# Reordered loads at the start and a reordered meeting of two stages in an AdaLN/FFN kernel on one core

## The chip, the cores and the metric

The kernel runs on one core of a Trainium2 chip. Its time is the device time of one execution, in microseconds; the median of several executions counts. The engines are TensorE (PE; its weight loads are listed apart as PEld), VectorE (DVE), ScalarE (ACT), GpSimd (POOL) and SyncE (SP), which here only issues transfers.

## The reference

x is (32, 64, 1024): 2048 tokens of 1024 features. It goes through two residual stages.

```python
x = x + L0_ffn(L0_cond(x))     # stage 0
x = x + L1_ffn(L1_cond(x))     # stage 1
# L0_cond: agg_w[b] = softmax(mlp(cond[b])) . weight[k];  out = agg_w @ x + agg_b   (64 x 64 per batch)
# L0_ffn:  r = softmax(x @ gate_w.T); ((x * (r @ in_scale)) @ sign(W).T) * (r @ out_scale) + bias
# L1_cond: grouped convolution, 4 groups, 9 taps over the 1024 positions, + ctx + bias
# L1_ffn:  x @ W.T + b, plus 8 gated low-rank terms: w_e = softmax_e(q_e . k_e), h_e = x @ A_e.T, sum of w_e h_e @ B_e.T
```

Everything is float32. Products are made in a reduced format from split operands: each float32 operand is a rounded high part and a rest (`hi`, `lo`), and two or three products of parts stand for one.

## The kernel before

The tokens are 16 tiles of 128 rows (two batches each), handled as 8 pairs; tile (i, p) is tile 2i + p. Every buffer that a tile needs exists twice, one for each p. Each engine has its own program written out in order, with loops over the pairs in the middle and the first and last pairs unrolled; the engines meet only through semaphores, on which an instruction waits until a count is reached. So an instruction that waits holds up all that stands behind it on its engine.

**Stage 0, one tile on PE**: `product_y` (64 small products, L425, bank from `agg` and the x tile in `xs`), `product_logits` (L438), `sum_logits` (L448), `turn_routing` (L455), `product_scales` (L467 and L473) and 32 `ffn0_step`s of 128x512 (L491). The small products of later tiles are put between the steps of the current one at fixed step numbers (`TURN_AT`, `BLOCK_AT`, `SUM_AT`). The first tile has its own list (k = 6, 10, 16, 22, 28): at k == 22 PE waits for the fourth tile of x, tile (1, 1), with `inputs_of_y(1, 1)`, and only then makes the logits of tile (1, 0). DVE adds the mix bias (L883), scales (L905), makes the rests (L912) and multiplies with the out scale (L920, semaphore `scaled`). POOL adds the bias row `bias_bc` to the second copy of x (`add_bias0`, L1059), adds the product (`make_x1`, L1066), and makes the rest of each chunk of `wearly`, the first weights of stage 1 (`rest_of_stage`, L1070). ACT rounds (`round_parts` L724, `round_stage` L738).

**SP, the one queue of nearly all transfers**: `load_next(i, p, biased)` waits until the tile that had the buffer has been used (`y_biased`), loads x into `xs` (L227) and the row for it (L232). `load_again(i, p)` loads x a second time into `resid`, which is part of `work` (L266); in the first pair these buffers held parts of the sign weights, so it waits for `signs_ready`. `replace_x1` stores the result of stage 0 to memory (`x1_scratch`, L287) and loads the next tile into the same buffer. `next_chunk` loads the next chunk of `wearly` once the last is split. `load_raw` (L336) reads a finished tile of `x1_scratch` back as 8 transfers into `raw`, the convolution's input.

**Where the stages meet**: in the last tile of stage 0, PE puts the first convolution (`product_conv(0, 2)`, 128 small products, L566) in front of step `CONV0_AT`. DVE adds the context (L991, L995) into `z_t`, ACT rounds it and DVE makes the rests (semaphores `z_biased`, `z_hi`, `z_lo`). PE then waits for `stage_hi[0]` and `stage_lo[0]` to reach 8 (all chunks of `wearly` split) and for `z_lo`, and starts `period1`: 48 steps of 128x320 (L587, q, k and A), the next convolution, 24 steps of 128x512 with `early`, the transposed gates and 24 steps with `late` weights that are themselves split only then (`late_hi` on ACT L801, `late_lo` on DVE L1008 and POOL L1096). After that all tiles run the same `period1`.

Of the kernel before, what the change touches and what calls it, by code (L numbers as in the profile page):

```python
# [32 lines left out]
P = 128  # L33
B, S, H = 32, 64, 1024
TILES = B * S // P
PAIRS = TILES // 2
L8 = H // P
# [19 lines left out]

TURN_AT, BLOCK_AT, SUM_AT, CONV0_AT = 7, 18, 26, 8
LORA_AT = 11
# [4 lines left out]
def adaln_ffn_kernel(nc, x, consts, rows, mix, wsign, scales, bias0, toep, wearly, wlate, bm, bias1, out):  # L64
# [6 lines left out]
    with ctx:  # L71
# [153 lines left out]
        def _(sp):  # L225
# [42 lines left out]
            sp.wait_ge(rows_stored, 16)  # L268
            load_next(1, 0, 2)
            for p in range(2):  # L270
                sp.wait_ge(signs_ready, 7 + p)
                load_again(0, p)
            sp.wait_ge(scale_ready, 1)
            sp.dma_start(bias_bc[:, :], bias0.broadcast_to([P, H])).then_inc(bias0_loaded, 16)
            load_next(1, 1, 4)

# [30 lines left out]

            late_i, last = PAIRS - 3, PAIRS - 1
            load_next(last, 1, 4 * late_i + 8)
            replace_x1(late_i, 0)  # L310
            next_chunk(late_i)
# [14 lines left out]

            def load_raw(i, p):

                sp.wait_ge(x1_stored[p], 16 * (i + 1))
                src = tile_rows(x1_dram, 2 * i + p).rearrange("(n c) (l q) -> l c n q", c=CG, l=L8)  # L330
                half = L8 // 2
                for lo in range(2):
                    for l in range(half):
                        part = (lo * half + l) * CG
                        at = 1 - lo
                        sp.dma_start(raw[part:part + CG, p, :, at:at + P],  # L336
                                     src[(1 - lo) * half + l]).then_inc(raw_loaded[p], 16)

            sp.wait_ge(pads_zeroed, 2)
            load_raw(0, 0)  # L340
            load_raw(0, 1)
# [40 lines left out]
        def _(pe):  # L382
# [206 lines left out]
            def period1(i, p, ni, q, late_ready=None):  # L589
# [4 lines left out]
                for h in range(2):  # L594
                    for k in range(24):
                        if h == 1 and k == 12 and ni is not None:
                            inputs_of_conv(ni, q)
                            if late_ready:

                                pe.wait_ge(out_scale_ready, 2 * TILES)  # L600
                            else:

                                pe.wait_ge(out_ready, 4 * i + 2 * p)
                        last = z_step(bank[2 + h][:, 0:NH], lambda b, c: early[:, b, c, h * NH:(h + 1) * NH], p, k)
                    last.then_inc(qk_done, 1)
# [28 lines left out]

            pe.wait_ge(stage_hi[0], 8)
            pe.wait_ge(stage_lo[0], 8)
            pe.wait_ge(stage_hi[1], 1)
# [27 lines left out]
        def _(act):  # L665
# [126 lines left out]
            period0(last, 0, (last, 1))  # L792
            period0(last, 1, None, None, last)

            act.wait_ge(ffn0_done, 2 * TILES - 2)
            round_parts(0, 0, z_t, z_biased, z_hi, by_token)

            act.wait_ge(ffn0_done, 2 * TILES)
# [256 lines left out]
        def _(pool):  # L1055
# [15 lines left out]


            def period0(before, now, chunk=None):

                make_x1(*before, 1)
                add_bias0(*now)
                if chunk is not None:
                    hi, lo = (early[:, a, bass.ds(chunk, 1), :].rearrange("p a n -> p (a n)") for a in range(2))
                    rest_of_stage(0, NW, chunk + 1, lo, hi)
                make_x1(*now, 0)  # L1080
# [6 lines left out]
            rest_of_stage(1, H, 1, lora[:, 1, :], lora[:, 0, :])  # L1087
            with pool.Fori(1, PAIRS) as i:
                period0((i - 1, 1), (i, 0))
                period0((i, 0), (i, 1), i)  # L1090
            last = PAIRS - 1
            make_x1(last, 1, 1)
            for k in (0, 2):
# [89 lines left out]
```

## Time and profile before

| what | value |
|---|---|
| median of 3 runs | 557.45 us (555.99 to 559.61) |
| the profiled execution | 560.03 us, of it span 558.0 us |
| PE busy | 538.6 us, 97% of the span |
| PEld, DVE, POOL, ACT busy | 83%, 46%, 28%, 22% |
| chain that ended last | PE 92%, DVE 3%, DMA 2%, ACT 1%, issue 1% |
| mean granted clock of PE | 0.991 |

The chain is followed back from the last instruction to what released it at each step. PE's busy time says that it had a matmul in flight; how fast those ran depends on the granted clock, which the views by windows give as a share of full speed.

### The profile page before, as it was taken

Reading aid. Unit: us, or ns where it says so; the run is one execution under the profiler, and the core shown is the slowest. Engines: PE = TensorE matmul, PEld = TensorE weight load, DVE = VectorE, ACT = ScalarE, POOL = GpSimd, SP = SyncE. Lnnn points to the kernel's source line nnn. Section 1 sums busy time; section 2 is a strip of 40 time slices with the busy share of each in tenths; the row PEclk is TensorE's granted clock in tenths of the full one; section 3 lists DMA queues with packets and bytes.
Section 4 is the critical chain, followed back from the end, with each engine's and each line's share of the span. In section 5 each row is a group of like instructions: output and inputs, shape, how many; then the busy total and the mean of one; then the engine's idle time right before and its main releaser. Section 6 shows DMA issues by size and latency. Waiting matters only on the chain.

```text
span 558.0 us, 13990 instructions
## 1 busy us (share of the span) xinstructions
PE 538.6 (97%) x5717; PEld 461.9 (83%) x5717; DVE 254.7 (46%) x461; ACT 123.4 (22%) x289; POOL 155.5 (28%) x79
## 2 busy tenths in 40 slices
PE   5879999999999899999999999999999999999997
PEld 4657788787887798898988988989889899898896
DVE  4439888797775762323224332242232322422321
ACT  5614434343434320101101011011011110110100
POOL 0027776767758490110101101011011010110100
PEclk9989999999999989999999999999999999999999
DMA  8684565555558451330412303204033032130100
GB/s 311 241 330 159 172 204 187 197 197 187 204 172 215 132 185 43 81 104 17 119 51 66 117 14 103 95 22 118 38 80 113 4 118 78 40 118 39 39 39 38
DMA packets 38775, 66.79 MB, mean 120 GB/s; under 512 B 4384, under 2 KB 25056, under 8 KB 38752
## 3 DMA queue, kind: packets, MB, share of 16 engines
q1 hardware_dynamic: 38528, 66.09, 36.3%
q10 hardware_dynamic: 224, 0.36, 0.3%
q8 instruction: 19, 0.31, 0.2%
q14 instruction: 4, 0.03, 0.0%
HBM read 49.64 MB, written 16.79 MB: 119 GB/s over the span
## 4 chain that ended last, share of the span: by engine, by line
PE 92%; DVE 3%; DMA 2%; ACT 1%; issue 1%; SPq 0%; DVEq 0%; ACTq 0%
PE bank L587 52%; PE bank L491 19%; PE bank L566 8%; PE bank L622 4%; PE bank L425 3%; DMA xs<-in_x 2%; PE bank L438 2%; PE bank L467 2%; DVE parts L912 1%; DMA cst<-in_consts 1%; ACT late L693 1%; PE bank L448 0%; PE bank L455 0%; PE bank L473 0%; ACT parts L724 0%
## 5 line engine op out<-in xcount | busy, mean ns | idle before, releaser
L587 PE MATMUL bank<-early,parts 128*128 128x320 f32 (+1 forms) x1152 | 208.2, 339 | 1.8 <-DVE parts L912 1.8
L587 PEld LDWEIGHTS bank<-early,parts 128*128 128x128 f32 x1152 | 186.1, 189 | 18.7 <-issue 2.2
L491 PE MATMUL bank<-late,parts 128*128 128x512 f32 x512 | 131.1, 408 | 1.5 <-ACT parts L724 1.5
L1101 POOL TENSOR_TENSOR work<-work,bias_bc 128x1024 f32<-128x1024 f32 x16 | 38.0, 2375 | 279.2 <-DMA work<-x_scratch 279.2
L491 PEld LDWEIGHTS bank<-late,parts 128*128 128x128 f32 x512 | 95.0, 193 | 22.6 <-ACT parts L724 1.7
L587 PE MATMUL bank<-late,parts 128*128 128x512 f32 x384 | 94.1, 394 | 0.0
L587 PEld LDWEIGHTS bank<-late,parts 128*128 128x128 f32 x384 | 70.9, 188 | 15.9
L912 DVE TENSOR_TENSOR parts<-y_t,parts 128x512 fp32r<-128x512 f32 x64 | 59.4, 931 | 12.3 <-ACT parts L724 11.0
L724 ACT ACTIVATE parts<-y_t 128x512 fp32r<-128x512 f32 x64 | 39.7, 633 | 98.7 <-DVE y_t L995 67.0
L1066 POOL TENSOR_TENSOR work<-work 128x512 f32<-128x512 f32 x32 | 45.9, 1436 | 49.4 <-DVE work L920 48.2
L1016 DVE TENSOR_TENSOR qk<-bank,qk 128x256 f32<-128x256 f32 x16 | 6.8, 425 | 104.6 <-ACT qk L810 104.6
L1059 POOL TENSOR_TENSOR work<-work,bias_bc 128x1024 f32<-128x1024 f32 x16 | 42.4, 2651 | 38.1 <-DMA bias_bc<-in_bias 33.8
L566 PEld LDWEIGHTS bank<-band,raw 64*64 64x64 f32 x2048 | 44.3, 134 | 3.2 <-issue 3.2
L566 PE MATMUL bank<-band,raw 64*64 64x128 f32 (+1 forms) x2048 | 46.5, 246 | 0.0
L1045 DVE TENSOR_TENSOR work<-bank,work 128x512 f32<-128x512 f32 x32 | 22.0, 688 | 41.0 <-PE bank L622 41.0
L1035 DVE TENSOR_TENSOR wh_t<-bank,wh_t 128x128 fp32r<-128x128 f32 x16 | 4.7, 292 | 76.0 <-ACT wh_t L818 76.0
L905 DVE TENSOR_TENSOR y_t<-bank,y_t 128x512 f32<-128x512 f32 x32 | 20.6, 686 | 26.7 <-PE bank L467 26.7
L808 ACT ACTIVATE qk<-bank 128x64 f32<-128x64 f32 x16 | 3.6, 223 | 111.2 <-PE bank L587 111.2
L622 PE MATMUL bank<-lora,wh_t 128*128 128x512 f32 x96 | 27.7, 396 | 0.0
L734 ACT ACTIVATE work<-bank 128x512 f32<-128x512 f32 x32 | 18.7, 587 | 23.8 <-POOL work L1066 23.8
L920 DVE TENSOR_TENSOR work<-bank,work 128x512 f32<-128x512 f32 x32 | 21.7, 681 | 4.7 <-PE bank L491 4.7
L991 DVE TENSOR_TENSOR y_t<-bank,row_bc 128x512 f32<-128x512 f32 x32 | 22.0, 688 | 3.5 <-PE bank L566 3.1
(91 smaller groups left out, 351.0 us busy)
## 6 DMA issues: line engine op xcount, KB each, us to landing
xs<-in_x SPq DMA_DIRECT2D x16, 512.0 KB, 3.4
work<-in_x SPq DMA_DIRECT2D x16, 512.0 KB, 3.3
x_scratch<-work SPq DMA_DIRECT2D x16, 512.0 KB, 3.0
raw<-x_scratch SPq DMA_DIRECT2D x128, 64.0 KB, 3.0
work<-x_scratch SPq DMA_DIRECT2D x16, 512.0 KB, 3.7
out_tokens<-work SPq DMA_DIRECT2D x15, 512.0 KB, 2.7
stage<-in_wearly SPq DMA_DIRECT2D x8, 576.0 KB, 3.9
row_bc<-token_rows_scratch SPq DMA_DIRECT2D x30, 64.0 KB, 3.2
```

Source lines behind the costliest of these rows:

```text
L491: last = mm(bank[4 + h][:, :], parts[:, p, a, c, :], signs[:, c, h * HALF:(h + 1) * HALF], start=(k % 16 == 0), stop=(k % 16 == 15))
L566: last = mm(into[g * S:(g + 1) * S, at + cols.start:at + cols.stop], raw[rows, p, n, s + g * S:s + (g + 1) * S], band[rows, s * GROUPS + n ...
L587: return mm(dst, parts[:, p, a, c, :], w(b, c), start=(k == 0), stop=(close and k == 23))
L622: last = mm(o[h][:, :], wh_t[:, a, :], lora[:, b, h * HALF:(h + 1) * HALF], start=False, stop=(k == 2))
L724: do(cols(parts[:, p, 0], h), cols(src, h), ACT.Copy).then_inc(done, 1)
L912: v.tensor_tensor(cols(parts[:, p, 1], h), cols(src, h), cols(parts[:, p, 0], h).bitcast(F32), ALU.subtract).then_inc(done, 1)
L920: v.tensor_tensor(o, bank[4 + h][:, :], o, ALU.mult).then_inc(scaled, 1)
L991: v.tensor_tensor(zt, by_group(bank[h]), add.broadcast_to([P, 4, L8, CG]), ALU.add).then_inc(conv_halved, 1)
L1045: v.tensor_tensor(o, bank[4 + 2 * p + h][:, :], o, ALU.add).then_inc(out_ready, 1)
L1059: g.tensor_tensor(resid[:, p, :], resid[:, p, :], bias_bc[:, :], ALU.add).then_inc(xb_ready, 2)
L1066: g.tensor_tensor(resid[:, p, cols], os_sb[:, cols], resid[:, p, cols], ALU.add).then_inc(x1_ready, 1)
L1101: g.tensor_tensor(resid[:, p, :], resid[:, p, :], bias_bc[:, :], ALU.add).then_inc(resid_ready, 1)
```

## The change

Four things are moved; nothing is computed that was not computed before.

- SP, start: the bias row and then `load_next(1, 1, 4)` are issued in front of the two `load_again(0, p)`, which were in front.
- SP, last pairs: `load_raw(0, 0)` is issued right behind the last `load_next`, that is in front of `replace_x1(5, 0)`; `load_raw(0, 1)` stays.
- PE: `CONV0_AT` is 4 instead of 8. The wait for the eighth chunk of `wearly` stands in front of step 21 of the first 24 steps of `period1` instead of in front of its first step, where 7 chunks are now enough.
- ACT and POOL, last pair: ACT rounds `z_t` of tile (0, 0) ahead of its work for stage 0's last tile and of the rounding of the last chunk. POOL waits for `z_lo` and splits the last chunk ahead of `add_bias0(7, 1)`; before, the chunk came behind it and waited for nothing but its rounding.

```diff
-TURN_AT, BLOCK_AT, SUM_AT, CONV0_AT = 7, 18, 26, 8
+TURN_AT, BLOCK_AT, SUM_AT, CONV0_AT = 7, 18, 26, 4
...
             load_next(1, 0, 2)
+            sp.wait_ge(scale_ready, 1)
+            sp.dma_start(bias_bc[:, :], bias0.broadcast_to([P, H])).then_inc(bias0_loaded, 16)
+            load_next(1, 1, 4)
             for p in range(2):
                 sp.wait_ge(signs_ready, 7 + p)
                 load_again(0, p)
-            sp.wait_ge(scale_ready, 1)
-            sp.dma_start(bias_bc[:, :], bias0.broadcast_to([P, H])).then_inc(bias0_loaded, 16)
-            load_next(1, 1, 4)
...
+            load_next(last, 1, 4 * late_i + 8)
             sp.wait_ge(pads_zeroed, 2)
             load_raw(0, 0)
+            replace_x1(late_i, 0)
+            next_chunk(late_i)
+            replace_x1(late_i, 1)
...
                     for k in range(24):
+                        if late_ready and h == 0 and k == 21:
+
+                            pe.wait_ge(stage_hi[0], 8)
+                            pe.wait_ge(stage_lo[0], 8)
...
-            pe.wait_ge(stage_hi[0], 8)
-            pe.wait_ge(stage_lo[0], 8)
+            pe.wait_ge(stage_hi[0], 7)
+            pe.wait_ge(stage_lo[0], 7)
...
-            period0(last, 1, None, None, last)
-
             act.wait_ge(ffn0_done, 2 * TILES - 2)
             round_parts(0, 0, z_t, z_biased, z_hi, by_token)
+            period0(last, 1, None, None, last)
...
-            with pool.Fori(1, PAIRS) as i:
+            with pool.Fori(1, PAIRS - 1) as i:
                 period0((i - 1, 1), (i, 0))
                 period0((i, 0), (i, 1), i)
             last = PAIRS - 1
+            period0((last - 1, 1), (last, 0))
+            make_x1(last, 0, 1)
+            pool.wait_ge(z_lo, 2)
+            split_chunk(last)
+            add_bias0(last, 1)
+            make_x1(last, 1, 0)
             make_x1(last, 1, 1)
```

How the instructions move on SP at the start of the program (the names are those above; `work<-in_x` is `load_again`, `xs<-in_x` the x tile of `load_next`; - is before, + is after):

```order
 L227 DMA xs<-in_x 128x1024
 L232 DMA row_bc<-token_rows_scratch 128x128
-L266 DMA work<-in_x 128x1024 x2
-L274 DMA bias_bc<-in_bias 128x1024
+L271 DMA bias_bc<-in_bias 128x1024
 L227 DMA xs<-in_x 128x1024
 L232 DMA row_bc<-token_rows_scratch 128x128
+L266 DMA work<-in_x 128x1024 x2
 L235 DMA stage<-in_bm 128x1024
 L235 DMA stage<-in_wearly 128x1152
```

The second `xs<-in_x` is the fourth tile of x; three transfers stood between it and the first, now one does, the bias row.

On POOL at the end of stage 0, before (the loop's last rows, and what followed it):

```order
L1059 TENSOR_TENSOR work<-work,bias_bc 128x1024
L1070 ISA
L1070 TENSOR_TENSOR early<-stage,early 128x1152
L1064 REGISTER_ALU
L1066 TENSOR_TENSOR work<-work 128x512
L1088 REGISTER_ALU
L1088 COMPARE_AND_BRANCH
L1066 TENSOR_TENSOR work<-work 128x512
L1096 TENSOR_TENSOR late<-late_raw,late 128x1024
L1096 TENSOR_TENSOR late<-stage,late 128x1024
```

and with the change, behind the loop that is now one round shorter:

```order
L1069 TENSOR_TENSOR work<-work 128x512
L1062 TENSOR_TENSOR work<-work,bias_bc 128x1024
L1069 TENSOR_TENSOR work<-work 128x512 x2
L1073 TENSOR_TENSOR early<-stage,early 128x1152
L1062 TENSOR_TENSOR work<-work,bias_bc 128x1024
L1069 TENSOR_TENSOR work<-work 128x512 x2
L1108 TENSOR_TENSOR late<-late_raw,late 128x1024
L1108 TENSOR_TENSOR late<-stage,late 128x1024
```

The split (`early<-stage,early`) of the last chunk now stands in front of the last bias addition (`work<-work,bias_bc`), not behind it.

## Rows read from the trace of the kernel before

**Rows 1.** Waits: engine and line, what it waited for; total us, times, longest.

```profile
PE bank L438 <- DMA xs<-in_x: 4.1, 1, 4.1
```

**Rows 2.** Timeline from the start: start us, us, engine, line, instruction, count.

```profile
22.11 1.28 DVE L883 TENSOR_TENSOR y_t<-bank,row_bc 128x512 f32<-128x512 f32 x2
...
23.93 1.27 SPq L266 DMA_DIRECT2D work<-in_x  x2
...
29.54 1.64 PE L491 MATMUL bank<-late,parts 128*128 128x512 f32 x6
...
30.33 0.33 SPq L227 DMA_DIRECT2D xs<-in_x  x1
```

**Rows 3.** Chain that ended last, in order of time: start us, us, what.

```profile
25.72 9.55 DMA xs<-in_x
...
35.96 1.63 PE bank L425 x64
...
38.63 2.86 PE bank L491 x6
...
58.98 1.09 PE bank L425 x64
...
60.67 2.02 PE bank L491 x8
```

**Rows 4.** Windows: us, busy (instructions) by engine, granted clock PEclk, DMA share, GB/s.

```profile
36.00:43.00 7.00, 7.00 (x86) 5.89 (x86) 3.21 (x7) 2.24 (x7) 1.83 (x2) 0.52 0.75 298
196.00:200.20 4.20, 4.20 (x20) 4.20 (x19) 4.20 (x4) 1.67 (x2) 4.09 (x3) 0.59 0.09 37
```

**Rows 5.** Timeline, DVE, after the fourth tile of x.

```profile
38.66 1.29 DVE L905 TENSOR_TENSOR y_t<-bank,y_t 128x512 f32<-128x512 f32 x2 [7.50 <-PE bank L467]
...
45.14 0.68 DVE L920 TENSOR_TENSOR work<-bank,work 128x512 f32<-128x512 f32 x1
```

**Rows 6.** Transfers issued at 20 to 23, 25.1 to 25.6 and 30 to 40 us; last, us to landing.

```profile
xs<-in_x SPq DMA_DIRECT2D x1, 512.0 KB, 3.3
...
bias_bc<-in_bias SPq DMA_DIRECT2D x1, 512.0 KB, 8.7
...
xs<-in_x SPq DMA_DIRECT2D x1, 512.0 KB, 9.2
```

**Rows 7.** Timeline from 146 to 174 us, SP and POOL, the last pairs of stage 0.

```profile
151.02 0.33 SPq L266 DMA_DIRECT2D work<-in_x  x1
...
159.22 2.40 POOL L1059 TENSOR_TENSOR work<-work,bias_bc 128x1024 f32<-128x1024 f32 x1
...
173.88 8.82 SPq L336 DMA_DIRECT2D raw<-x_scratch  x16
```

**Rows 8.** Timeline from 179 us on, where the stages meet.

```profile
179.94 5.29 PE L491 MATMUL bank<-late,parts 128*128 128x512 f32 x22
...
181.50 1.30 DVE L912 TENSOR_TENSOR parts<-y_t,parts 128x512 fp32r<-128x512 f32 x2 [0.16 <-ACT parts L724]
...
185.16 2.91 PE L566 MATMUL bank<-band,raw 64*64 64x128 f32 x128
...
189.42 2.40 POOL L1059 TENSOR_TENSOR work<-work,bias_bc 128x1024 f32<-128x1024 f32 x1 [3.85 <-DMA work<-in_x]
189.66 5.78 DVE L912 TENSOR_TENSOR parts<-y_t,parts 128x512 fp32r<-128x512 f32 x2
...
191.78 3.10 POOL L1070 TENSOR_TENSOR early<-stage,early 128x1152 f32 x1
...
195.58 8.81 PE L587 MATMUL bank<-early,parts 128*128 128x320 f32 x48 [1.84 <-DVE parts L912]
...
202.93 2.38 POOL L1096 TENSOR_TENSOR late<-stage,late 128x1024 fp32r<-128x1024 f32 x1
```

**Rows 9.** Chain, first and second tile of stage 1.

```profile
207.23 5.67 PE bank L587 x24
...
219.88 7.03 PE bank L587 x48
```

More of the change, by code:

```diff
@@ L308, in _, with load_raw @@
             late_i, last = PAIRS - 3, PAIRS - 1
+            def load_raw(i, p):
+                sp.wait_ge(x1_stored[p], 16 * (i + 1))
+                src = tile_rows(x1_dram, 2 * i + p).rearrange("(n c) (l q) -> l c n q", c=CG, l=L8)
+                half = L8 // 2
+                for lo in range(2):
+                    for l in range(half):
+                        part = (lo * half + l) * CG
+                        at = 1 - lo
+                        sp.dma_start(raw[part:part + CG, p, :, at:at + P],
+                                     src[(1 - lo) * half + l]).then_inc(raw_loaded[p], 16)
             load_next(last, 1, 4 * late_i + 8)
+            sp.wait_ge(pads_zeroed, 2)
+            load_raw(0, 0)
             replace_x1(late_i, 0)
@@ L325, in _ @@
             next_chunk(last - 1)
[L327 to L340, printed above, removed]
             load_raw(0, 1)
@@ L1070, in rest_of_stage, with split_chunk @@
                 g.tensor_tensor(dst, stage[:, p, 0:n], hi.bitcast(F32), ALU.subtract).then_inc(stage_lo[p], 1)
+            def split_chunk(chunk):
+                hi, lo = (early[:, a, bass.ds(chunk, 1), :].rearrange("p a n -> p (a n)") for a in range(2))
+                rest_of_stage(0, NW, chunk + 1, lo, hi)
             def period0(before, now, chunk=None):
@@ L1077, in period0 @@
                 if chunk is not None:
-                    hi, lo = (early[:, a, bass.ds(chunk, 1), :].rearrange("p a n -> p (a n)") for a in range(2))
-                    rest_of_stage(0, NW, chunk + 1, lo, hi)
+                    split_chunk(chunk)
                 make_x1(*now, 0)
```

## The prediction

> **What bounds the kernel now.** I read the chain that ended last first: 92% of it is PE, so only time in which PE stands still or runs slowly counts. Then the waits: PE's longest wait for anything is 4.1 us for the fourth tile of x [rows 1]. Then the timeline around it and around the meeting of the stages, where PE stands 1.84 us for DVE's rests of the first stage-1 tile [rows 8]. Last the windows, for the granted clock: from 36 to 43 us it is 0.52 on average, and from 196 to 200.2 us 0.59 [rows 4]; outside such stretches it is 1.00. Both slow stretches begin about a us after one of the two stalls has ended. The lower of the clock's two levels is 1.2 GHz, the upper 2.4 GHz. So each stall has cost twice: the wait, and matmuls at half clock behind it.
>
> **Part 1, the start.** PE has done its step group at 29.54 + 1.64 = 31.18 us [rows 2] and can go on when the fourth tile has landed. It was issued at 25.72 and took 9.55 us, to 35.27 [rows 3]. What held the issue back was not the buffer: the rows of the second tile were biased at 22.11 + 1.28 = 23.39 us, but SP stood in front of the two second loads, issued from 23.93 on [rows 2], and the bias row. Now only the bias row is in front, and it is issued during SP's idle time, at about 21 us. So the fourth tile is issued at about 23.5, 2.2 us earlier, and has 1 MB less in front of it.
>
> When it lands is the unknown. The same load in a nearly empty queue took 3.3 us [rows 6]: 26.8. With everything of before around it, it took 9.55: 33.05. In between, if it has to wait for the bias row, whose broadcast took 8.7 us [rows 6], that is 21 + 8.7 = 29.7. I take 27 to 30: what stood in front of it and is now behind is two of the four large transfers. That is before 31.18, so the whole 4.1 us goes. The Trainium skill (DMA: Bandwidth & Descriptors, Queues, rings and completion order) says that each DMA engine takes descriptors in ring order, though transfers need not complete in that order. By this rule the loads now behind the tile don't hold it, and the time is the forecast's; the trace neither shows nor excludes it, since the long landings [rows 6] fit a queue that shares its rate too. What would follow if it shares is the third rival.
>
> The half clock goes with the stall. The 7 us from 36 to 43 at 0.52 are 7 x 0.48 = 3.4 us of full-clock work at most. At the rows: 64 small products took 1.63 against 1.09 us, 6 steps took 2.86 against 6/8 of 2.02 = 1.52 [rows 3]. That is 0.5 + 1.3 us in 4.5 us, so 2.4 to 3.4 over the stretch; I take 3.2, as most of it was large steps.
>
> Not all of 4.1 + 3.2 = 7.3 is kept. DVE starts its chain for tile (0, 1) when PE has made the scales (38.66) and ends it with the out scale (45.14 + 0.68 = 45.82), 7.2 us later [rows 5], work that a faster PE clock hardly shortens. That start moves by 4.1 + about 1.0 (the half clock up to 38.66) = 5.1 us, PE's steps by 7.3. PE has no wait for DVE there now; how near it is, no row says. So 0 to 2.2 us are given back, and I take 0.6. **Part 1: 6.7 us, bounds 4.5 to 7.5.**
>
> The second loads come out about 0.5 us later on SP. POOL alone waits for them and its first addition was held by the bias row, issued behind them and 8.7 us under way, which now lands earlier; cost nothing. If that cover is gone, POOL's x1 is late and ACT's copy of the next out scale with it.
>
> **Part 2, eight raw loads moved ahead on SP.** The 16 took 8.82 us of SP [rows 7], so 8 are 4.4. They now stand in front of a store and the reload of `resid` for tile (6, 0), which was issued at 151.02: at worst 155.4, landed 3.4 later at 158.8. POOL uses it at 159.22 [rows 7]. Hidden, but by 0.4 us only; uncovered, POOL moves by what is missing and PE is not next in line, since two more instructions stand between. Behind the stage's last loads SP gets 4.4 us back: the reload of tile (7, 1), for which POOL stood 3.85 us [rows 8], lands earlier.
>
> **Part 3, the meeting.** The convolution moves by four steps of 5.29 / 22 = 0.24 us, so it begins at 185.16 - 0.96 = 184.2 and everything of `z_t` is 0.96 us earlier; PE's own sum is the same and the last step ends at 195.58 - 1.84 = 193.74 as before. Its condition, all of the last tile's `u` scaled, is met before DVE's rests of it begin at 181.50 [rows 8].
>
> DVE's two rests took 5.78 us, to 195.44, beside POOL's 2.40 and 3.10 us; two of the same shape took 1.30 at 181.50 [rows 8]. So beside POOL they are four times slower. POOL now waits for `z_lo` between its last `make_x1` and the split, so it is idle then: the rests are done at 189.66 - 0.96 + 1.3 and some 0.2 for ACT, about 190.2. PE is ready at 193.74: the 1.84 us go, with 3.5 us to spare.
>
> The split is late next. ACT rounds the last chunk behind `z_t`, at about 191, POOL takes 3.10 at worst: 194.1 to 195. PE asks for it at step 21 of 48, 21 x 7.03 / 48 [rows 9] = 3.1 us after 193.74, at 196.8. Nearly 2 us to spare. Behind it on POOL stand the bias, two `make_x1` and the two late rests, that ended at 202.93 + 2.38 = 205.3 [rows 8]. POOL begins at most 1.8 us later than its 189.42, so 207.1 at worst; PE needs them at 207.23 + 5.67 = 212.9 [rows 9] less 3.6 = 209.3. Hidden by 2.2 us. The Trainium skill (GPSIMD Engine Reference, Specifications) says that GpSimd's SBUF interfaces are shared with VectorE, and that instructions with two SBUF inputs contend. The rests above agree, and the rule speaks against the change as well: DVE's late rests have two SBUF inputs too, and now meet POOL's moved additions. By it they are longer, and the time is the second rival's. Final stores and the second bias row are moved a few us behind work that is 10 us from its use: nothing.
>
> The half clock after this stall: the first 48 steps took 8.81 [rows 8], later ones 7.03 [rows 9]: 1.8 us. **Part 3: 1.84 + 1.78 = 3.6 us, bounds 1.8 to 3.7.** Everything after runs as before, with PE full.
>
> **Sum.** 6.7 + 3.6 = 10.3 us. The profiled execution took 560.03 (span 558.0 and 2.03 around it): 549.7. The median shown is 557.45, 2.6 lower, which would give 547.2. The three runs lie 3.6 us apart, and stalls on a transfer and the clock's return are what I expect to vary; as they go, part of the 2.6 goes too. I put the time at 548.0, about a third of the way.
>
> **Rivals.**
> 1. *The tile still comes late* (chance 0.17). Only the issue moves and the landing keeps its 9.55 us: 33.05. PE stands 1.9 us, about as long as at the meeting, where the half clock then cost 1.8. Part 1 is 4.1 - 1.9 + 3.2 - 1.8 = 3.6 instead of 6.7: 551.1. For it: the three landings issued from 25 to 31 us took 8.7 us or more [rows 3, 6]. Against: they all had the 1 MB in front.
> 2. *The meeting gets another wait* (0.05). DVE's late rests and POOL's moved additions slow each other, so that the last late rest ends after 209.3, or ACT rounds the chunk late, and PE stands at step 21 or ahead of the late steps; the 3.6 us come back: 551.6. Against: 2 us to spare at each.
> 3. *The transfers share the rate, and the tile lands last* (0.04). With bias row, second loads and stage-1 weights all in flight it lands only when the one issued at 30.33 does, 30.33 + 9.2 = 39.5 [rows 2, 6]. Then PE stands 8.3 us, 4.2 more than now. Part 3 gives 3.6 back: 0.6 us slower than before, 558.1, and slower still if part 3 fails. It decides against the change from a landing of 35.27 + 3.6 = 38.9 us on. Against: the tile before it landed in 3.3 us, and at 298 GB/s [rows 4] the 2 MB behind it alone are 7 us.
>
> That the change does nothing is excluded at the meeting by its order, and at the start is the first rival's extreme.
>
> **Chances and range.** Under 1% of 557.45, 5.6 us, a measurement can't tell from no change; the line is at 551.9. The forecast holds 0.74. Its own range is the bounds of the parts, 546.0 to 551.0. With rival 1 and half of 2 the range is 545.5 to 552.0, with some 0.15 outside. Faster by over 1%: nearly all of the 0.74, 0.12 of rival 1, 0.02 of rival 2, together 0.87. Same: 0.11. Slower by over 1%: 0.02, rival 3 with a failed meeting.
>
> **What the profile will show.** Right: no wait of PE's L438 for `xs`; no window near 36 to 43 us with a clock under 1.00; the bias row and the fourth tile issued at about 21 and 23.5 us; the first 48 steps of L587 in about 7.0 us, right behind PE's last L491; L912 for `z_t` at 0.7 us each. Wrong: a PE wait of over 1 us for `xs` (rival 1 or 3), a wait in front of step 21 or of the late steps (rival 2), or a half clock without a stall in front of it, which would leave the waits' 6.0 us as the whole gain and 552.

## The result: 551.04 us against 557.74, faster by 1.1%

| | before | changed |
|---|---|---|
| median of 4 runs | 557.74 us (555.99 to 559.61) | 551.04 us (550.01 to 551.41) |
| ratio, 95% interval | | 0.9891 (0.9864 to 0.9917) |
| profiled execution, its span | 560.03, 558.0 us | 550.01, 548.2 us |
| mean granted clock in it | 0.991 | 0.999 |

The time is inside the range of the prediction (545.5 to 552.0), 3.0 us over its 548.0; the range that the forecast's own parts gave, 546.0 to 551.0, just misses it, and what covers it is the width that was added for the first two rivals. The profiled executions differ by 10.0 us, close to the forecast's sum of 10.3; the medians differ by 6.7. The agreement of the profiles is in part luck: at 560.03 us the profiled execution of before is slower than each of the 50 executions of that kernel that were timed later (553.43 to 559.17). That difference is the case's lesson, and most of the experiments are about it.

The changed kernel's start, by its timeline (columns as in [rows 2]; L886, L908, L915, L1062, L1069 and L1073 are before's L883, L905, L912, L1059, L1066 and L1070):

```profile
23.41 0.33 SPq L227 DMA_DIRECT2D xs<-in_x  x1
...
30.68 0.64 PE L438 MATMUL bank<-y_t,cst 128*32 128x128 f32 x16
...
41.72 1.16 ACT L742 ACTIVATE early<-stage 128x1152 fp32r<-128x1152 f32 x1
...
42.77 0.27 ACT L708 ACTIVATE logits_t<-bank 128x128 f32<-128x128 f32 x1
...
43.14 0.33 PE L467 MATMUL bank<-routing_t,scale_w 32*128 32x128 f32 x2 [0.89 <-issue]
...
49.44 0.33 PE L455 MATMUL bank<-cst,routing 128*128 128x128 f32 x1 [0.41 <-ACT routing L717]
```

The fourth tile is issued at 23.41 (forecast 23.5). Its transfer, in the view of transfers for that moment:

```profile
xs<-in_x SPq DMA_DIRECT2D x1, 512.0 KB, 4.5
```

It landed at 27.9, inside the 27 to 30 that was taken, and the wait of [rows 1] is gone: PE makes the logits at 30.68, 4.6 us earlier than at 35.3. Of the 4.6 us, 0.4 were there before the stall: the third 64 products started at 26.52 instead of 26.93, and the experiments show that this moment varies. The bias row took 5.5 us instead of 8.7.

What is given back shows at 43.14: PE stands 0.89 us, and nothing in the profile but ACT's copy of the logits (42.77 + 0.27) ends just before it. The copy stood behind the rounding of a chunk of weights, and both behind a copy of the out scale at 41.23, which waited for POOL's `make_x1` and that for DVE's out scale. The wait of 0.41 us at 49.44 is not new; the kernel before had it too:

```profile
55.57 0.33 PE L455 MATMUL bank<-cst,routing 128*128 128x128 f32 x1 [0.39 <-ACT routing L713]
```

Windows (columns as in [rows 4]), the first slow one and then 190 to 200 us, where the kernel before has a clock of 0.84 on average:

```profile
36.00:43.00 7.00, 6.25 (x101) 4.80 (x99) 6.92 (x11) 3.98 (x9) 3.15 (x2) 1.00 0.78 299
190.00:200.00 10.00, 10.00 (x171) 9.25 (x170) 6.05 (x10) 2.94 (x7) 9.14 (x5) 1.00 0.70 233
```

And the meeting of the stages, for [rows 8]:

```profile
178.05 2.91 PE L566 MATMUL bank<-band,raw 64*64 64x128 f32 x128
...
182.55 1.47 DVE L915 TENSOR_TENSOR parts<-y_t,parts 128x512 fp32r<-128x512 f32 x2
...
184.98 2.66 POOL L1073 TENSOR_TENSOR early<-stage,early 128x1152 fp32r<-128x1152 f32 x1 [5.62 <-ACT early L742]
187.37 7.20 PE L587 MATMUL bank<-early,parts 128*128 128x320 f32 x48
```

PE goes from the last step of stage 0 into the 48 steps without a stall, and they take 7.2 us instead of 8.81. DVE's two rests take 1.47 us instead of 5.78 and are done 3.3 us before PE asks.

From the two profiles: the convolution began at 185.16 and now at 178.05, of which 0.96 is its own move, so the start is worth 6.15 us (forecast 6.7), with the 0.4 of the earlier clock in it; the whole span is 9.8 shorter, which leaves 3.65 for the meeting (forecast 3.6).

### The profile page after: what moved, and what is told of

Read it like the earlier page. It is cut to its first block, busy times and chain, and to the rows that moved or that the text cites. A ratio compares the mean times of both kernels' runs of the same rounds, so it can differ in the third digit from the quotient of the medians.

```text
span 548.2 us, 13985 instructions
## 1 busy us (share of the span) xinstructions
PE 533.6 (97%) x5717; PEld 457.7 (83%) x5717; DVE 250.8 (46%) x461; ACT 123.1 (22%) x289; POOL 155.4 (28%) x79
## 4 chain that ended last, share of the span: by engine, by line
PE 96%; DVE 1%; ACT 1%; issue 1%; DMA 0%; DVEq 0%; ACTq 0%
PE bank L587 53%; PE bank L491 22%; PE bank L566 8%; PE bank L626 4%; PE bank L425 4%; PE bank L438 2%; PE bank L467 2%; DVE parts L915 1%; DMA cst<-in_consts 0%; PE bank L448 0%; PE bank L455 0%; PE bank L619 0%; PE bank L473 0%; DVE y_t L908 0%; DVE y_t L886 0%
## 5 line engine op out<-in xcount | busy, mean ns | idle before, releaser
L491 PE MATMUL bank<-late,parts 128*128 128x512 f32 x512 | 128.7, 403 | 1.5 <-ACT parts L728 1.5
L491 PEld LDWEIGHTS bank<-late,parts 128*128 128x128 f32 x512 | 93.3, 190 | 22.0 <-ACT parts L728 1.7
L587 PE MATMUL bank<-late,parts 128*128 128x512 f32 x384 | 94.1, 394 | 0.0
L587 PEld LDWEIGHTS bank<-late,parts 128*128 128x128 f32 x384 | 70.9, 188 | 16.0
L915 DVE TENSOR_TENSOR parts<-y_t,parts 128x512 fp32r<-128x512 f32 x64 | 56.3, 881 | 12.4 <-ACT parts L728 11.0
L1069 POOL TENSOR_TENSOR work<-work 128x512 f32<-128x512 f32 x32 | 46.8, 1464 | 45.7 <-DVE work L923 44.5
L1062 POOL TENSOR_TENSOR work<-work,bias_bc 128x1024 f32<-128x1024 f32 x16 | 42.8, 2674 | 30.3 <-DMA work<-in_x 30.3
L908 DVE TENSOR_TENSOR y_t<-bank,y_t 128x512 f32<-128x512 f32 x32 | 20.6, 686 | 22.4 <-PE bank L467 22.4
```

The lines of the kernel that those rows point to most:

```text
L491: last = mm(bank[4 + h][:, :], parts[:, p, a, c, :], signs[:, c, h * HALF:(h + 1) * HALF], start=(k % 16 == 0), stop=(k % 16 == 15))
L587: return mm(dst, parts[:, p, a, c, :], w(b, c), start=(k == 0), stop=(close and k == 23))
L915: v.tensor_tensor(cols(parts[:, p, 1], h), cols(src, h), cols(parts[:, p, 0], h).bitcast(F32), ALU.subtract).then_inc(done, 1)
L1062: g.tensor_tensor(resid[:, p, :], resid[:, p, :], bias_bc[:, :], ALU.add).then_inc(xb_ready, 2)
L1069: g.tensor_tensor(resid[:, p, cols], os_sb[:, cols], resid[:, p, cols], ALU.add).then_inc(x1_ready, 1)
```

## The experiments

Each was timed in turns with the kernel before, on one chip for the kernels of a group. In the three groups the kernel before had medians of 556.45 (28 runs), 556.82 (11) and 556.41 us (11).

**Start alone** (`e1_start_only`).

```diff
             load_next(1, 0, 2)
-            for p in range(2):
-                sp.wait_ge(signs_ready, 7 + p)
-                load_again(0, p)
             sp.wait_ge(scale_ready, 1)
             sp.dma_start(bias_bc[:, :], bias0.broadcast_to([P, H])).then_inc(bias0_loaded, 16)
             load_next(1, 1, 4)
+            for p in range(2):
+                sp.wait_ge(signs_ready, 7 + p)
+                load_again(0, p)
```

> The kernel before with the start alone changed: bias row and fourth tile of x issued in front of the two second loads. My theory (the 4.1 us stall and the half clock behind it go, about 1 us is given back in the chain over DVE, POOL and ACT): 6.1 us less in a profiled execution, no PE wait on the fourth tile, granted clock 1.00 from 36 to 43 us, and the stall of 1.8 us with a half clock behind it still there at the meeting of the stages. As the medians of the two kernels differ by only 6.7 us, the median here should fall by 3.5 to 6. Rival (the slow clock is not the stall's doing but comes at this time of the program anyway): 3 us less, the window from 36 to 43 us still near 0.5.

Measured: 552.84 us (552.11 to 554.78, 11 runs), ratio 0.9937 (0.9920 to 0.9954): 3.6 us. In the profiled execution, the slowest of the 11 and 5.3 us under that of before (expected 6.1), there is no wait for the tile and the clock is 1.00 from 36 to 43 us. At the meeting PE stood 2.02 us and the half clock followed:

```profile
187.14 3.09 POOL L1070 TENSOR_TENSOR early<-stage,early 128x1152 f32 x1
...
190.33 8.81 PE L587 MATMUL bank<-early,parts 128*128 128x320 f32 x48 [2.02 <-issue]
```

The release is not DVE's: its two rests ran from 184.24 for 3.50 us and were done at 187.7. PE starts 0.1 us after POOL's split of the last chunk, 187.14 + 3.09 = 190.23. The other 10 executions have mean clocks of 0.999 and 1.000, though nothing in this kernel takes the stall at the meeting away.

**Meeting alone** (`e2_meeting_only`): the changed kernel with the opposite of the diff above.

> The changed kernel with the start put back as it was before: raw loads, first convolution, PE's wait, ACT's and POOL's order at the meeting are those of the change. My theory: 3.6 us less than before (1.84 of stall, 1.78 of half clock), first 48 steps of stage 1 in about 7.0 us; the stall on the fourth tile and the slow window at 36 to 43 us as before. The two parts add up: this and the start alone together give the whole change to within 0.7 us. Rival (the parts share something, e.g. the clock's state): they don't add up, the sum is over 1.5 us more or less than the whole.

Measured: 554.90 us (551.92 to 556.96, 12 runs), 0.9976 (0.9951 to 1.0001): 1.6 us, with an interval that just reaches no difference, and not the 3.6 that were expected. With the start's 3.6 that is 5.2, and the whole change gave 5.4 beside them: the parts add up, as far as intervals of 1 to 1.5 us to either side can tell. But "the slow window as before" was wrong for the profiled execution. It stood 3.09 us for the tile and went on at full clock:

```profile
33.99 0.64 PE L438 MATMUL bank<-y_t,cst 128*32 128x128 f32 x16 [3.09 <-DMA xs<-in_x]
34.57 1.16 PE L425 MATMUL bank<-agg,xs 64*64 64x64 f32 x64
```
```profile
36.00:43.00 7.00, 7.00 (x39) 5.64 (x35) 6.49 (x13) 3.59 (x8) 1.21 (x2) 1.00 0.84 314
```

So a stall may or may not be followed by the half clock. The tile was issued at 25.43 and took 8.53 us, so it landed 1.3 us earlier than in [rows 3] though the code is the same there. PE's wait of about 0.9 us in front of the scales is there as well (0.87 us at 45.84): it comes when the half clock is gone, whatever the start.

**PE at work through the stall** (`e3_filled_stall`).

```diff
                 if k == 22:
+                    pe.wait_ge(out_scale_ready, 2)
+                    for f in range(17):
+                        mm(bank[7][:, :], parts[:, 0, 0, f % 4, :], signs[:, f % 4, 0:HALF], start=True, stop=True)
                     inputs_of_y(1, 1)
```

> The kernel before, with 17 matmuls of 128x512 into a bank that is free (about 4 us of work whose result nothing reads) in front of PE's wait for the fourth tile of x; all transfers as before. PE works through the stall instead of standing. Theory: the wait stays as long (PE resumes at about 35.3 us), but the granted clock stays at 1.00 from 36 to 43 us, and the time falls by the half clock's 3.2 us less up to 1 us given back: 2.2 to 3.2 us less than before. Rival (the clock falls for another reason than PE's standing still, e.g. the full transfer queues at that time): no gain, or a loss of up to 0.5 us, and the window still at 0.5.

Measured: 555.90 us (554.73 to 558.07, 12 runs), 1.0006 (0.9986 to 1.0027): the same as before, where 2.2 to 3.2 us less was expected, so by the time the theory missed. In the profiled execution the added work ended at 30.58 + 4.04 = 34.62, just as the tile landed (issued at 25.57, 9.0 us), so there it was as long as the stall. In an execution whose tile lands as early as 33.96 the same work is too long; that this ate up the gain in the median is argued and not shown. What is shown is that at full clock this kernel's median is 555.49 us, 1.5 over that of before. The clocks do answer: 8 of 12 executions at 0.999 or 1.000 and none below 0.996, against 8 of 50 and down to 0.990 for the kernel before. By the profile 36 to 43 us is at 1.00. So the half clock behind the first stall goes with PE's standing still; the rival's full transfer queues were there too, with a DMA share of 0.90 in that window. At the meeting the profile shows again what PE stood for, and that a stall of 2.55 us need not cost clock (7.28 us for the 48 steps):

```profile
186.77 1.48 DVE L915 TENSOR_TENSOR parts<-y_t,parts 128x512 fp32r<-128x512 f32 x2
188.32 2.40 POOL L1062 TENSOR_TENSOR work<-work,bias_bc 128x1024 f32<-128x1024 f32 x1 [5.63 <-DMA work<-in_x]
190.68 2.62 POOL L1073 TENSOR_TENSOR early<-stage,early 128x1152 f32 x1
...
193.40 7.28 PE L590 MATMUL bank<-early,parts 128*128 128x320 f32 x48 [2.55 <-issue]
```

DVE's rests were over at 188.25, uncontended, and PE stood until POOL's split ended at 193.30. POOL had stood 5.63 us for the reload.

**The change again** (`e4_after_again`).

> The changed kernel again, beside the others on the same chip. Theory: as measured, 0.989 of before (0.986 to 0.992), 5.6 to 7.5 us less; the profile again near 9.8 us under the one shown of before if that one was at the slow end of its spread, or nearer 7 us if the profile shown of the changed kernel was at its fast end. Rival (the forecast's 10.3 us is what the change is worth and the first medians were low by chance): 9 to 10.5 us less in the median too.

Measured: 551.08 us (550.13 to 552.71, 6 runs), 0.9917 (0.9888 to 0.9946), and a profiled execution of 550.13. The medians, lower in their gain than the forecast, were not chance.

All executions, in groups by the mean granted clock of each (medians in us, number of executions):

| | 0.999 to 1.000 | 0.996, 0.997 | 0.993, 0.994 | 0.990, 0.991 | mean clock |
|---|---|---|---|---|---|
| before | 553.96 (8) | 556.38 (21) | 556.77 (17) | 558.58 (4) | 0.9955 |
| start alone | 552.68 (10) | 554.78 (1) | | | 0.9995 |
| meeting alone | 552.74 (3) | 554.37 (2) | 555.07 (5) | 556.59 (2) | 0.9954 |
| whole change | 550.96 (9) | 552.71 (1) | | | 0.9994 |

The clock comes in steps of about 0.003, and over the 50 executions of before a step goes with 3 x 0.40 = 1.2 us (straight line through all). Read across: at full clock the whole change is worth 3.0 us; the mean clock is another 0.0039, 1.6 us by that line, and nearly all of that belongs to the start, since the meeting alone doesn't move it. The two are 4.6 of the 5.4 us. The line is a rough price, as the groups of before are 2.4, 0.4 and 1.8 us apart: by them, the median of all 50 (556.45) is 2.5 us over the group at full clock. By the profile of before, where 5.0 us of half clock went with 0.009, it would be 2.2 us (an estimate). So the clock is worth some 1.6 to 2.5 us in the median. A group differs from another by more than its clock, since an earlier landing can make the stall shorter too; no run takes the two apart. The profile on which the prediction rests, 560.03 us at 0.991, belongs to the slowest group.

The half clock at the meeting is rare: with the start alone, 10 of 11 executions ran at full clock. And not every drop belongs to these stalls: of the 53 executions of the change and its variants below, whose profiles show neither stall, 6 had a mean clock of 0.994 to 0.997.

**ACT's copy first** (`f5_logits_first`), to get back the 0.89 us.

```diff
                 copy_out_scale(i, p, 1)
+                if first:
+                    copy_logits(*two)
                 if chunk is not None:
                     round_stage(...)
-                if two:
+                if two and not first:
                     copy_logits(*two)
```

> The changed kernel, with ACT copying the logits of tile (1, 1) ahead of rounding the first chunk of stage-1 weights (in the first period only), instead of behind it. In the changed kernel's profile PE stands 0.89 us at 42.26 in front of the scales, until ACT's copy at 42.77 is done. Theory (that is where most of the 0.96 us given back went): the wait goes and the time falls by 0.6 to 0.9 us against the changed kernel, to about 550.2. Rival (the give-back is DVE's chain beside POOL, and PE then waits at the transposed routing instead): the wait at 42.3 goes and the one at 49.4, 0.41 us, grows by as much; time the same within 0.2.

Measured: 550.74 us (550.61 to 551.61, 4 runs), 0.9890 (0.9867 to 0.9912). It is the rival that came: the wait in front of the scales is gone, and the one at the routing is 1.31 us instead of 0.41. DVE's rest in between now runs wholly beside POOL's split and takes 2.78 instead of 1.84 us.

```profile
43.63 0.33 PE L467 MATMUL bank<-routing_t,scale_w 32*128 32x128 f32 x2
...
45.42 2.70 POOL L1075 TENSOR_TENSOR early<-stage,early 128x1152 fp32r<-128x1152 f32 x1
45.89 2.78 DVE L917 TENSOR_TENSOR parts<-y_t,parts 128x512 fp32r<-128x512 f32 x1 [0.16 <-ACT parts L728]
...
51.01 0.32 PE L455 MATMUL bank<-cst,routing 128*128 128x128 f32 x1 [1.31 <-ACT routing L717]
```

This profile is not directly comparable with that of the change, as its third 64 products start 1.15 us later (27.67 and 26.52). The kernel with the raw loads back, below, starts them at 27.61: there the scales come at 44.69 after a wait of 0.97 us and the routing at 51.00, here at 43.63 and 51.01. So the copy's place moves the scales by 1.06 us and the routing not at all.

**The edits at the meeting, one by one.** POOL's old order (`f6_pool_old_order`):

```diff
-            with pool.Fori(1, PAIRS - 1) as i:
+            with pool.Fori(1, PAIRS) as i:
...
-            period0((last - 1, 1), (last, 0))
-            make_x1(last, 0, 1)
-            pool.wait_ge(z_lo, 2)
-            split_chunk(last)
-            add_bias0(last, 1)
-            make_x1(last, 1, 0)
```

> The changed kernel with POOL's order at the meeting as before: bias addition for tile (7, 1), then the split of the last chunk, no wait for the rests of the first stage-1 tile. Theory: with the raw loads moved and the convolution earlier, POOL's additions still run beside DVE's two rests, which take 2 to 3 us each again instead of 0.7, but begin 1 us earlier than before; PE waits 0 to 1 us at its first step, time 0 to 1 us more than the changed kernel. Rival (POOL's bias addition is done before DVE's rests start, because the reload it waited for now lands 4 us earlier, so that only the split runs beside them): no wait at all, time the same.

Measured: 550.83 us (550.35 to 551.10, 4 runs), 0.9894 (0.9871 to 0.9917): as the rival said, no wait. The reload landed for POOL at 179.84 and its bias addition was over before the rests began:

```profile
179.84 2.40 POOL L1062 TENSOR_TENSOR work<-work,bias_bc 128x1024 f32<-128x1024 f32 x1 [0.38 <-DMA work<-in_x]
...
182.65 1.48 DVE L915 TENSOR_TENSOR parts<-y_t,parts 128x512 fp32r<-128x512 f32 x2
```

Convolution at step 8 (`f7_conv_at_8`):

```diff
-TURN_AT, BLOCK_AT, SUM_AT, CONV0_AT = 7, 18, 26, 4
+TURN_AT, BLOCK_AT, SUM_AT, CONV0_AT = 7, 18, 26, 8
```

> The changed kernel with the first convolution in front of step 8 again instead of step 4. Everything of the first stage-1 tile is 0.96 us later. Theory: DVE's rests end at about 185.0 instead of 184.0 by the changed kernel's profile and PE asks for them at 187.4, so nothing waits; time the same as the changed kernel (within 0.3 us). Rival (the shift of the convolution is what took the wait away): a wait of about 1 us and the time up by 1.

Measured: 550.98 us (550.05 to 552.78, 6 runs), 0.9903 (0.9881 to 0.9924), no wait, as the theory said. But POOL's split of the last chunk, which the theory left out, ended after PE's start at 187.64:

```profile
186.16 2.68 POOL L1073 TENSOR_TENSOR early<-stage,early 128x1152 fp32r<-128x1152 f32 x1 [6.52 <-ACT early L742]
```

Its end, 188.84, is 1.2 us behind PE's start, which PE's moved wait allows. With the wait for the eighth chunk in its old place PE would have stood there.

Raw loads back (`g12_raw_loads_back`):

```diff
             load_next(last, 1, 4 * late_i + 8)
-            sp.wait_ge(pads_zeroed, 2)
-            load_raw(0, 0)
...
+            sp.wait_ge(pads_zeroed, 2)
+            load_raw(0, 0)
             load_raw(0, 1)
```

> The changed kernel with all 16 raw loads in their old place on SP, everything else as in the change. Theory: POOL's additions stand behind its wait for the rests, so they can't slow them even with a late reload; the bias addition comes after the split anyway; no stall, time the same as the changed kernel within 0.3 us. Rival (the order on SP is what took the stall away in the change itself): a stall of 1 us or more in front of stage 1, or POOL's late rests too late for PE at about 203 us.

Measured: 550.77 us (549.98 to 551.55, 5 runs), 0.9894 (0.9870 to 0.9918), no stall, as the theory said. The reload is issued 1.2 us after the convolution begins (180.75 and 179.59) instead of 0.6 us before it, and POOL, which has the split first, is not held by it.

ACT's old order (`g13_act_old_order`):

```diff
+            period0(last, 1, None, None, last)
             act.wait_ge(ffn0_done, 2 * TILES - 2)
             round_parts(0, 0, z_t, z_biased, z_hi, by_token)
-            period0(last, 1, None, None, last)
```

> The changed kernel with ACT's order as before: out scale and rounding of the last chunk ahead of the rounding of the first stage-1 tile. Theory: ACT is done with the chunk before it is asked for the tile (in the kernel before it ended 1.1 us before the tile came), and with the convolution 1 us earlier it comes just out even, so at most 0.3 us are lost and nothing reaches PE: time the same. Rival (ACT's chunk now stands in front of the tile): the rests are 1 us later, still in front of PE; only if they end after 187.4 us is there a stall.

Measured: 550.51 us (549.63 to 552.89, 6 runs), 0.9903 (0.9876 to 0.9929), no stall, as the theory said.

The raw loads alone (`g11_raw_loads_only`): the start of the change, and at the meeting only this edit of it:

```diff
             load_next(last, 1, 4 * late_i + 8)
+            sp.wait_ge(pads_zeroed, 2)
+            load_raw(0, 0)
...
-            sp.wait_ge(pads_zeroed, 2)
-            load_raw(0, 0)
             load_raw(0, 1)
```

> The changed start, and of the four edits at the meeting only the first 8 raw loads moved ahead on SP; convolution at step 8, PE's, ACT's and POOL's order and waits as before. Theory (the raw loads alone did it: the reload that POOL stood 3.85 us for lands early, POOL's bias addition is over before DVE's rests of the first stage-1 tile begin, and only the split of the last chunk can meet them): PE's stall in front of stage 1 falls from 1.8 to 0 to 0.5 us and the time is that of the changed kernel, within 0.5 us. Rival (the split, rounded by ACT early as before, now runs beside the rests and holds them instead): rests of 2 to 3 us, a stall of 1 to 2 us, 1 to 2 us over the changed kernel.

Measured: 551.05 us (550.27 to 554.72, 6 runs), 0.9915 (0.9885 to 0.9945), no stall, as the theory said. POOL's chain is over 3 us before PE asks for it (the view ends at 193 us, so the last row has 35 of the 48 steps):

```profile
179.97 2.41 POOL L1059 TENSOR_TENSOR work<-work,bias_bc 128x1024 f32<-128x1024 f32 x1
...
182.34 2.69 POOL L1070 TENSOR_TENSOR early<-stage,early 128x1152 f32 x1
...
184.09 2.08 DVE L912 TENSOR_TENSOR parts<-y_t,parts 128x512 fp32r<-128x512 f32 x2
...
188.01 5.29 PE L587 MATMUL bank<-early,parts 128*128 128x320 f32 x35
```

**A warm clock from the start.** Up to 24 us PE's durations are those of the lower clock in every profile above, though the clock column reads 1.00 there. Two kernels give it work in the gaps; first a large set (`f8_idle_work`):

```diff
+            def idle_work(n, cols=HALF):
+                for f in range(n):
+                    mm(bank[5][:, 0:cols], cst[:, 0:P], cst[:, 0:cols], start=True, stop=True)
+            idle_work(2)
             pe.wait_ge(att_tiled, 1)
...
             first_rows(1)
+            pe.wait_ge(tok_rows_ready, 2)
+            idle_work(1, P)
             product_logits(0, 0, True)
+            idle_work(1, P)
             sum_logits(0, 0, True)
...
             pe.wait_ge(scale_ready, 1)
+            idle_work(1)
             product_scales(0, 0, True)
+            idle_work(2)
```

> The changed kernel with matmuls that nothing reads put where PE stands in the first 21 us: two of 128x512 while it waits for the attention weights, two of 128x128 around the first logits, one of 128x512 in front of the first scales and two behind them. In all profiles so far PE's durations up to 24 us are those of the lower clock (64 products in 1.92 us against 1.09 later; 6 steps in 2.93 against 1.5), and the moment at which they change, seen in the start of the third 64 products at 26.5 to 27.5 us, varies by 1 us. Theory: more work in the gaps brings the clock up earlier, the third 64 products start 1 to 3 us earlier, and the time falls by 0.5 to 3 us against the changed kernel, with a smaller spread. Rival (the added work is not enough, or is itself on the path): the clock comes at the same time and the time rises by the overshoot, 0.5 to 1.5 us.

Measured: 553.69 us (553.15 to 555.24, 6 runs), 0.9947 (0.9927 to 0.9967) of before: 2.6 us more than the change. The clock did rise earlier, by 22.3 us (the scales took 0.33 instead of 0.47 us, the 6 steps 1.78 instead of 2.93). But the first two matmuls stand as four in the profile, together 3.78 us in a gap of 1.8, and put 2.5 us on the path:

```profile
6.35 3.78 PE L398 MATMUL bank<-cst 128*128 128x512 f32 x4 [0.75 <-DMA cst<-in_consts]
...
10.06 0.79 PE L402 MATMUL bank<-wh,rws 32*128 32x128 f32 x2
...
24.49 1.78 PE L496 MATMUL bank<-late,parts 128*128 128x512 f32 x6
```

Then a set that fits (`g9_two_gaps`):

```diff
             pe.wait_ge(scale_ready, 1)
+            pe.wait_ge(tok_rows_ready, 2)
+            idle_work(1, 256)
             product_scales(0, 0, True)
+            idle_work(1)
```

> The changed kernel with matmuls that nothing reads in two of the early gaps only: one of 128x256 in front of the first scales (a gap of 0.8 us) and one of 128x512 behind them (a gap of 1.5 us, to 21.5 us). The larger set of such matmuls brought the clock up by 22.3 us instead of 25 to 27, but two of them stood on the path and cost 2.5 us. Theory: the added work fits the gaps, the clock comes up at about the same earlier time, 6 steps from 21.5 us take 1.8 instead of 2.9 us, and the time falls by 0.5 to 1.5 us against the changed kernel, to 549.5 to 550.5. Rival (it was the long first matmuls that brought the clock up): the clock comes as in the changed kernel, the time is the same or up by 0.3.

Measured: 550.78 us (550.20 to 553.28, 6 runs), 0.9906 (0.9881 to 0.9931): the same as the change; the expected 0.5 to 1.5 us did not come, though the clock did. The 6 steps took 1.66 us and PE made the next logits 1.2 us early (23.20 instead of 24.37), and then it stood for ACT:

```profile
21.23 1.66 PE L495 MATMUL bank<-late,parts 128*128 128x512 f32 x6 [0.46 <-ACT parts L735]
...
26.03 0.36 PE L452 MATMUL bank<-cst,logits_t 128*128 128x8 f32 x2 [1.06 <-ACT logits_t L715]
26.32 1.16 PE L429 MATMUL bank<-agg,xs 64*64 64x64 f32 x64
```

The third 64 products start at 26.32, and at 26.52 in the changed kernel. ACT's copy of the logits stands behind its rounding of the sign weights, and that chain sets the pace here. No version tried beats the change beyond its spread.

**What the start of the upper clock is worth.** How early the upper clock came shows in the start of the third 64 products. In the profiles of the change, of its repeat and of the kernels with POOL's order, the convolution, ACT's order or the two gaps edited, six in all, they start at 26.3 to 27.2 us, and the execution takes 550.0 to 550.4. In the two in which they start at 27.61 and 27.67 (raw loads back, copy first) it takes 551.55 and 551.61, and the timeline has a wait that the six don't have:

```profile
27.67 1.16 PE L425 MATMUL bank<-agg,xs 64*64 64x64 f32 x64
...
41.30 0.73 PE L491 MATMUL bank<-late,parts 128*128 128x512 f32 x2 [0.41 <-DVE work L925]
```

The whole difference between the change and raw loads back (1.54 us) is there by the first convolution (178.05 and 179.59). So part of the spread of the change's executions goes with the moment at which the upper clock comes, as far as eight profiles show.

## Why the prediction held, and where it was off

**The start's mechanism: right, one row misread.** SP's two second loads held the issue, it moved by 2.3 us, the tile landed in 4.5 us, the stall and the slow window went, and 0.97 us was given back in the chain over DVE, POOL and ACT (taken 0.6, bounds 0 to 2.2). The transfers now behind the tile did not hold it up to PE's need at 30.68. The Trainium skill's rule (DMA: Bandwidth & Descriptors, Queues, rings and completion order) that was weighed agrees with that landing after 4.5 us. "PE has no wait for DVE there now; how near it is, no row says" is not what the trace of before says: PE stood 0.39 us at 55.57 for ACT's routing, behind DVE's rests, so the chain over DVE was already the one that set the time there. The routing moved from 55.57 to 49.44, by 6.13 us; PE's logits before it moved by 7.10 (47.62 to 40.52), and the 0.97 between the two went into the new wait at 43.14. The kernel with the copy first moved that wait to the routing and won nothing. In the prediction's terms the stall was 4.1, the half clock 3.07 in place of 3.2 (from 35.31 to 47.62 us in before against 33.99 to 43.23 in the same work of the meeting alone), the give-back 0.97. The 0.4 of the earlier clock and a pause of some 0.6 us within the 64 products at 31.26 nearly cancel; what PE paused for there is open.

**The size of the clock term: wrong, for the median.** "So each stall has cost twice" is the step. The 3.2 and 1.8 us were read rightly from an execution in which both happened, 4 of 50 such. Over all executions of before the mean clock is 0.9955, and what the change returns of it is some 1.6 to 2.5 us in place of 5.0. The 1.8 of the meeting is hardly in it, as 10 of 11 executions of the start alone, which leaves that stall in the program, kept the full clock. The forecast was put "about a third of the way" from 547.2 (the median less 10.3) to 549.7 (the profile less 10.3). That named the right reason and gave it too little: with it the forecast should have been 549.7 or above. The rest of the miss is in the waits. At full clock the change is worth 3.0 us in the median, while the profiles' waits less the give-back are 4.1 + 1.8 - 1.0 = 4.9. In the meeting alone's profile the tile landed 1.3 us earlier than in before's, and 0.7 earlier in that with PE at work, so the landing varies by as much and before's profile has the longest stall of the three. And the change's profiled executions, 550.01 and 550.13, are at the low end of its own 550.01 to 552.71; part of that is the upper clock's early start in them, the rest is open. That the measured 551.04 is also the first rival's 551.1 is chance.

**The meeting: right result, half of the wait seen.** The profile and the prediction put PE's 1.84 us down to DVE's rests, which ended last, at 195.44; POOL's split ended at 191.78 + 3.10 = 194.88, 0.56 us before, and I did not count it as the same wait. With the rests done at 187.7 and 188.25, PE still stood 2.0 and 2.5 us, until POOL's split was done at 190.23 and 193.30. The root is the reload of tile (7, 1) behind the 16 raw loads: it held POOL's bias addition, that the split, and both ran beside the rests. The prediction saw the reload's 4 us as a side effect of part 2; with the changed start the raw loads by themselves are enough. Putting back any one of four edits (raw loads, convolution, POOL, ACT) costs nothing either; that one of the others alone would be enough was not tested. PE's later wait for the eighth chunk was not put back alone, and it is not idle: in the change the split ended at 184.98 + 2.66 = 187.64, 0.3 us after PE had started at 187.37, and 1.2 us after with the convolution at 8. It was over before PE's start with ACT's old order (186.85) and with the raw loads alone (185.03). That contention would move to DVE's late rests (rival 2) did not happen: they take 1.52 and 1.86 us in the change and 1.93 and 2.29 in the kernel before.

**The rivals.** Rival 1 asked for a PE wait on the tile and there is none in any profile with the changed start; its time, 551.1, is the one measured, by another mechanism. Rival 2 asked for a wait at step 21 or ahead of the late steps, and there is none. Rival 3 is refuted by the landing at 27.9.

## What to carry to other kernels

Where a stall is followed by a half clock in the profile, count the wait in full and the clock by how often it falls, from the clocks of several executions, not from the one profiled. Before naming the engine that a start waits for, list all of its conditions and the end of each: one that ends 0.5 us earlier is the next wait, and the earliest common cause (here a queue of small transfers in front of one reload) is the cheapest edit. PE work made only to keep or raise the clock paid in none of three tries here: once it did not fit the gap, once another engine set the pace, and once the median did not move though the clock did.

## What was not expected of the hardware

- Stalls of 4.1, 2.0 and 1.8 us were followed by a half clock (a mean of 0.83 and 0.84 over 190 to 200 us at the meeting, 8.81 us for the 48 steps in both), others of 3.1 and 2.55 us were not. The length of a stall alone does not decide.
- The fourth tile's transfer, with the same queue around it, took 9.55 us in one execution and 8.53 in another (ended at 35.27 and 33.96).
- The granted clock reads 1.00 up to 24 us where 64 products take 1.92 us instead of 1.09; there the durations tell the clock, not the column.
